# Attention stage: a group's choice of experts run one slot later, woven between the operations that add the next group's attention

## The chip, the core and the metric

The kernel runs on one core of a Trainium2 chip. Its metric is the device time of one execution in microseconds, as the median of several runs. The engines of the core have a queue each and work through it strictly in order: the matmul engine (PE in the profile), the Vector engine (DVE), the Scalar engine (ACT), GpSimd (POOL), and SP, which here only issues DMAs. Engines wait for each other, and an engine for its own earlier results, by semaphores.

## The reference

Four residual layers over 4096 tokens of width 128: linear attention, a mixture of 8 experts, a token mix with a decaying scan, and the same experts again. What the change touches is the attention and the choice of one expert for each token that follows it.

```python
def attn(x):                                 # x: 4 x 1024 x 128, normed
    q, k = elu(x @ W_q) + 1, elu(x @ W_k) + 1
    v = x @ W_v
    S, z = running sums over t of k_t v_t^T and of k_t
    return ((S_t q_t) / max(z_t . q_t, 1e-6)) @ W_o

def ffn(x):                                  # x normed
    logits = x @ router_W + router_b
    top1 = argmax(softmax(logits))           # one expert of 8
    gate = softmax(logits)[top1]
    return gate * (relu(x @ W1[top1] + b1[top1]) @ W2[top1] + b2[top1])

x = x + attn(layernorm(x))
x = x + ffn(layernorm(x))
x = x + mix(layernorm(x))
x = x + ffn(layernorm(x))
```

## The kernel before

The order on each engine is written out by hand. The 4096 tokens are 32 tiles of 128, and 4 tiles are a group (`GT = 4`, `NG = 8` groups). The attention stage is a software pipeline of slots k = 0 to 8: each engine has a function `attn_slot(k)` that does for several groups the steps whose turn it is.

In slot k PE does, in this order: `project_qk(k)` (L1271), `project_out(k-2)` (L1349, which gives the attention's output y of group k-2 with its denominator and its part of the logits), `score(k-1)` (L1286), `turn_kv(k-1)` (L1298, L1301), `transpose_x(k+1)` (L1246), the prefix counts `count` of group k-3 (L1256, L1260), `updates(k-1)` (L1310), `read_intra(k-1)` (L1321), `read_inter(k-1)` (L1332) and `project_v(k)` (L1276). Slot 8 has no `project_qk` and no `project_v`.

In slot k DVE does: the addition of the attention to the rows of group k-2, that is `dmax` (L891, which waits for y), `rden` (L894), `lnew` (L899) and four rows operations (L904); the moments of these rows (`stats` L802, L807); `mask_scores(k-1)` (`am`, L913); `add_state(k-1)` (L921 or L924); `placed(k-3)` (L867 to L878); `phi(k)` (L932); `scan_z(k)` (L939); and then `choose(k-2)`, which has eight small steps in a chain, each on the result of the one before it: `lsum` L836, `ls` L844, `lg` L847, `mx` L849, `ld` L852, `rv` L855, `top` L857, `oh` L858. In slot 8 the steps of the expert table (`slot_table`, first L1062) come right after `am`.

`read_intra(k-1)` needs `am(k-1)`, and `am(k-1)` stands on DVE's queue behind the addition and the moments of group k-2, hence behind y of group k-2.

POOL does in slot k: `z_dot_q(k-1)` (L484, reads two tiles of 64x512 in SBUF), `old_logits(k-2)` (L490), `row_scales(k-2)` (L476, waits for the moments through ACT's L619), and four indirect DMAs (L502), the second half of group k-4 and the first half of group k-3. In the kernel before, `z_dot_q(k-1)` also waits until `oh` of group k-3 is there (`after(pool, AS["oh"], k - 2)`). ACT copies and activates what PE made, and takes the exponential of `ld` (`lexp`, L612).

Of the kernel before, what the change touches and what calls it, by code (L numbers as in the profile page):

```python
# [5 lines left out]
ALU = mybir.AluOpType  # L6
# [6 lines left out]
P = 128  # L13
# [32 lines left out]
def after(eng, sem, n):  # L46

    if n > 0:
        eng.wait_ge(sem, n)
# [11 lines left out]
def hybrid_block(nc, x, w_q, w_k, w_v, w_o, time_decay, mix_v, mix_r, rw_v, rw_r, rw_o,  # L61
# [41 lines left out]
    with ExitStack() as ctx:  # L103
# [199 lines left out]
        def per_tile(a, n):  # L303
            return a.unsqueeze(2).to_broadcast([P, n, E])
# [111 lines left out]
        def _(pool):  # L416
# [123 lines left out]
            for k in range(NG + 1):  # L540
                if k == 2:
                    scales(AS, len(NORM_BATCHES) - 1)

                after(pool, AS["oh"], k - 2)
                if 0 <= k - 1 < NG:
                    z_dot_q(k - 1)
                if k == NG:
                    send(0, AS, k - 4, 1)
                if k - 2 >= 0:
                    old_logits(k - 2)  # L550
                    row_scales(AS, k - 2)
                if 4 <= k < NG:
                    send(0, AS, k - 4, 1)
                if k - 3 >= 0:
                    send(0, AS, k - 3, 0)
# [20 lines left out]
        def _(act):  # L576
# [44 lines left out]
            def phi_parts(g):  # L621
                act.wait_ge(AS["qkp"], g + 1)

                after(act, AS["phi"], g)
                nc.scalar.activation(ex[:], bank[1][:], ACT.Exp)
                nc.scalar.activation(rl[:], bank[1][:], ACT.Relu).then_inc(AS["rel"], 1)
# [38 lines left out]
            def attn_slot(k):  # L665
                if k < NG:
                    phi_parts(k)
                if k - 3 >= 0:
                    lexp(0, AS, k - 3)
                if 0 <= k - 1 < NG:  # L670
                    evac_kv(k - 1)
                if k == 0:

                    evac_xT(AS, 1, "vp")
                    turned_weights()
                    evac_v(0)
                    router_weights()
                    norm(AS, 2)
                    return
                if k == NG:  # L680
                    evac_o(k - 1)
                    row_veps(AS, k - 2)
                    copy_w1(0, 0)
                    return
                if k + 1 < NG:
                    evac_xT(AS, k + 1, "vp")
                if k - 2 >= 0:
                    row_veps(AS, k - 2)
                if k + 2 < NG:
                    norm(AS, k + 2)  # L690
                if 0 <= k - 1:
                    evac_o(k - 1)
                evac_v(k)
# [102 lines left out]
        def _(dve):  # L796
# [14 lines left out]
                dve.wait_ge(s_x_in[g], 16 * (l + 1))  # L811
                moments((AS, BS)[l], 1, g)

            def choose(l, S, b, half=None):

                t = span(ROUTE_BATCHES[b])
                n = GT * len(ROUTE_BATCHES[b])
                steps = 5 if l == 0 else 4
                done = [steps * b + (3 if l == 0 else 2) * (half == 1)]

                def step(ins):
                    done[0] += 1
                    ins.then_inc(s_route[l], 1)
                    dve.wait_ge(s_route[l], done[0])

                rev = rev8[:].unsqueeze(1).to_broadcast([P, n, E])
                if half != 1:
                    logits_of(l, S, b, t, n, step)
                if half != 0:
                    argmax_of(S, b, t, n, rev, step)  # L830

            def logits_of(l, S, b, t, n, step):
                dve.wait_ge(S["rs2"], b + 1)
                if l == 0:
                    dve.wait_ge(AS["lold"], ROUTE_BATCHES[b][-1] + 1)
                    step(nc.vector.tensor_tensor(lsum[:, t], lnew[:, t], lold[:, t], ALU.add))  # L836
                    sums = lsum[:, t]
                elif b == LASTB:
                    dve.wait_ge(S["lnew"], 1)
                    sums = lnew[:, t]  # L840
                else:
                    dve.wait_ge(S["logits"], ROUTE_BATCHES[b][-1] + 1)
                    sums = bank[6][:, 0:n * E].rearrange("p (j e) -> p j e", e=E)
                nc.vector.tensor_tensor(ls[:, t], sums, per_tile(column(RSTD, t), n), ALU.mult  # L844
                                        ).then_inc(S["lgs"], 1)
                dve.wait_ge(S["lgs"], b + 1)
                step(nc.vector.tensor_tensor(lg[:, t], ls[:, t], rtb[:].unsqueeze(1).to_broadcast([P, n, E]),  # L847
                                             ALU.add))
                step(nc.vector.tensor_reduce(mx[:, t], lg[:, t], AX_X, ALU.max))  # L849

            def argmax_of(S, b, t, n, rev, step):
                nc.vector.tensor_tensor(ld[:, t], lg[:, t], per_tile(mx[:, t], n), ALU.subtract  # L852
                                        ).then_inc(S["lead"], 1)
                dve.wait_ge(S["lead"], b + 1)
                step(nc.vector.scalar_tensor_tensor(out=rv[:, t], in0=ld[:, t], scalar=0.0, in1=rev,  # L855
                                                    op0=ALU.is_equal, op1=ALU.mult))
                step(nc.vector.tensor_reduce(top[:, t], rv[:, t], AX_X, ALU.max))  # L857
                nc.vector.tensor_tensor(oh[:, t], rev, per_tile(top[:, t], n), ALU.is_equal).then_inc(S["oh"], 1)  # L858

            def placed(l, S, b):  # L860

# [23 lines left out]
            def by_bank(a):  # L885
                return a.rearrange("p (b j) -> p b j", b=2)

            def denominators(g):
                t = tiles(g)
                dve.wait_ge(AS["y"], g + 1)  # L890
                nc.vector.tensor_scalar(by_bank(dmax[:, t]), outs[:, :, :, D], 1e-6, None, ALU.max  # L891
                                        ).then_inc(AS["dmax"], 1)
                dve.wait_ge(AS["dmax"], g + 1)
                nc.vector.reciprocal(rden[:, t], dmax[:, t]).then_inc(AS["rden"], 1)  # L894

            def add_attention(g):
                t = tiles(g)
                dve.wait_ge(AS["rden"], g + 1)
                nc.vector.tensor_tensor(lnew[:, t].rearrange("p (b j) e -> p b j e", b=2), outs[:, :, :, D + 1:YC],  # L899
                                        by_bank(rden[:, t]).unsqueeze(3).to_broadcast([P, 2, 2, E]), ALU.mult  # L900
                                        ).then_inc(AS["lnew"], 1)
                for j in range(GT):
                    v = val(g * GT + j)
                    last = nc.vector.scalar_tensor_tensor(out=v, in0=outs[:, j // 2, j % 2, 0:D],  # L904
                                                          scalar=rden[:, g * GT + j:g * GT + j + 1], in1=v,
                                                          op0=ALU.mult, op1=ALU.add)
                last.then_inc(AS["xnew"], 1)

            def mask_scores(g):
                dve.wait_ge(AS["scores"], g + 1)  # L910
# [31 lines left out]

            def attn_slot(k):

                if 0 <= k - 2:
                    denominators(k - 2)
                    add_attention(k - 2)
                if k == NG:

                    mask_scores(k - 1)  # L950
                    slot_table(0, 0, (0, 1))
                    add_state(k - 1)
                    slot_table(0, 0, (2,))
                if 0 <= k - 2:
                    dve.wait_ge(AS["xnew"], k - 1)
                    moments(AS, 2, k - 2)
                if 0 <= k - 1 < LASTG:
                    mask_scores(k - 1)
                    if k == 1:
                        mix_weights(1)  # L960
                    add_state(k - 1)
                if k - 3 >= 0:
                    placed(0, AS, k - 3)
                if k == NG:
                    return
                phi(k)
                scan_z(k)
                if k - 2 >= 0:
                    choose(0, AS, k - 2)
                if k < 2:  # L970
                    first_moments(0, k + 6)
                if k == 0:
                    mix_weights(0)
# [140 lines left out]
            def experts(l):  # L1114
# [39 lines left out]
                final = len(STAGES) - 1  # L1154
                dve.wait_ge(s_w2, 16 * (1 + E))
                if l == 0:
                    denominators(LASTG)
                    add_attention(LASTG)
                    norm_rows(0)
                else:  # L1160
                    norm_rows(0)
                    add_mix(LASTG)
# [428 lines left out]
```

## Time and profile before

| | us |
|---|---|
| median of 3 runs | 324.19 |
| lowest and highest run | 323.43, 325.46 |
| span of the profiled execution, first to last instruction | 351.4 |
| attention slots 2 to 8 in it, from the first to the last `dmax` | 23.30 to 74.69 |
| granted clock of the matmul engine in 26.8 to 77.0 | 1.00 |

The profiled execution gives no other time of its own than its span, which is 27.2 us longer than the median. The profile names a line as L904, an engine's idle time stands in brackets behind the instruction that ended it, and a count as x4 says that four instructions were merged into one row. The stage of interest is the attention, from about 5 to 83 us.

### The profile page before, as it was taken

The page shows a single profiled execution, that of the slowest core. Times are in us where ns is not written, and L with a number is a line of the kernel's source. Part 1 is how long each engine was busy: PE and PEld are TensorE (multiplying, and loading weights), DVE is VectorE, ACT ScalarE, POOL GpSimd, SP SyncE. Part 2 cuts the span into 40 slices and gives each one's busy share as a digit, 9 for nine tenths or more (in the row PEclk, how much of TensorE's full clock was granted, in tenths as well). Part 3 has the DMA queues.
Part 4 walks back from the last instruction along what each step waited for, and adds up shares of the span by engine and source line. Part 5 has one row for each costly group of instructions (what it writes and reads, how often), then busy time and mean ns, then how long its engine had stood idle before and what let it go on. Part 6 is the DMA issues. An engine that isn't in the chain of part 4 may idle for free.

```text
span 351.4 us, 9045 instructions
## 1 busy us (share of the span) xinstructions
PE 298.9 (85%) x2177; PEld 259.3 (74%) x2177; DVE 243.1 (69%) x1012; ACT 188.3 (54%) x545; POOL 205.9 (59%) x244
## 2 busy tenths in 40 slices
PE   7899998898948799999998978797976599989970
PEld 7566666655838799999945857686866499989960
DVE  4888989897563476877617999689453367777740
ACT  3865654323753576777604834423654377677730
POOL 4853688887565345545427867888483544544550
PEclk9999999999996899999999999968996899999995
DMA  7999010012223333310026000112212343321100
GB/s 194 272 322 142 20 34 31 31 33 79 64 62 94 76 79 82 90 52 32 23 67 172 2 16 15 48 39 79 67 59 78 79 87 83 89 57 40 33 7 0
DMA packets 32530, 25.72 MB, mean 73 GB/s; under 512 B 6000, under 2 KB 28785, under 8 KB 32480
## 3 DMA queue, kind: packets, MB, share of 16 engines
q1 hardware_dynamic: 27328, 16.51, 20.0%
q0 software_dynamic: 4576, 8.54, 7.4%
q8 instruction: 20, 0.33, 0.4%
q14 instruction: 30, 0.25, 0.2%
q10 hardware_dynamic: 576, 0.10, 0.2%
HBM read 14.57 MB, written 11.53 MB: 74 GB/s over the span
## 4 chain that ended last, share of the span: by engine, by line
PE 54%; DVE 15%; issue 9%; POOL 6%; another core or an unknown queue 5%; ACT 4%; DMA 2%; DVEq 1%; POOLq 0%; ACTq 0%; SPq 0%
PE pair L1496 19%; PE pair L1486 12%; PE bank L1486 6%; DVE stats L802 3%; PE bank L1474 2%; PE pair L1408 2%; POOL rstd L464 2%; PE pair L1349 1%; PE pair L1310 1%; PE pair L1321 1%; DVE rows L904 1%; DVE ys L1149 1%; PE pair L1276 1%; PE pair L1415 1%
## 5 line engine op out<-in xcount | busy, mean ns | idle before, releaser
L1496 PE MATMUL pair<-w2s,hT 128*128 x624 | 88.5, 287 | 3.5 <-issue 2.4
L1496 PEld LDWEIGHTS pair<-w2s,hT 128*128 128x128 f32 x624 | 80.1, 201 | 6.2 <-issue 5.8
L502 POOL DMA_INDIRECT sorted<-rows,place x64 | 68.5, 1071 | 26.8 <-issue 16.9
L1486 PE MATMUL pair<-xsT,w1s 128*128 128x128 f32 x432 | 62.2, 283 | 2.7 <-ACT xsT L740 2.1
L515 POOL DMA_INDIRECT out<-ys,xs x39 | 38.2, 981 | 40.3 <-DVE ys L1149 21.8
L515 POOL DMA_INDIRECT x_mid<-ys,xs x39 | 38.3, 983 | 39.2 <-DVE ys L1149 22.1
L1486 PEld LDWEIGHTS pair<-xsT,w1s 128*128 128x128 f32 x432 | 56.0, 198 | 3.7 <-issue 3.4
L1149 DVE SCALAR_TENSOR_TENSOR ys<-pair,xs 128x128 f32<-128x128 f32 x78 | 27.2, 349 | 43.3 <-PE pair L1496 24.9
L663 ACT COPY w1s<-w1all 128x516 f32 x78 | 49.0, 628 | 6.8 <-issue 3.4
L740 ACT COPY xsT<-bank 128x128 f32<-128x128 f32 x78 | 20.9, 268 | 58.7 <-PE bank L1474 31.9
L1128 DVE SCALAR_TENSOR_TENSOR xs<-b2b,xs 128x128 f32<-128x128 f32 x78 | 27.5, 352 | 21.4 <-DVE xsn L1120 15.0
L1486 PE MATMUL bank<-xsT,w1s 128*128 128x128 f32 x192 | 30.7, 295 | 11.9 <-issue 6.6
L1486 PEld LDWEIGHTS bank<-xsT,w1s 128*128 128x128 f32 x192 | 26.9, 209 | 13.1 <-issue 7.4
L1138 DVE TENSOR_SCALAR hT<-pair,w1s 128x128 f32<-128x128 f32 x112 | 34.1, 343 | 0.9 <-PE pair L1486 0.8
L802 DVE BATCH_NORM_STATS2 stats<-rows 128x6 f32<-128x128 f32 x128 | 27.5, 277 | 10.0 <-DMA rows<-x_mid 6.1
L746 ACT ACTIVATE hT<-pair,w1s 128x128 f32<-128x128 f32 x104 | 31.5, 375 | 1.1 <-issue 0.5
L746 ACT ACTIVATE hT<-bank,w1s 128x128 f32<-128x128 f32 x96 | 29.3, 379 | 0.0
L1120 DVE TENSOR_SCALAR xsn<-xs 128x128 f32<-128x128 f32 x78 | 27.0, 348 | 0.3
L476 POOL TENSOR_TENSOR rows<-veps,neg_half 128x4 f32<-128x4 f32 x16 | 18.5, 1159 | 9.6 <-ACT veps L619 9.4
L1474 PE MATMUL bank<-ident,xsn 128*128 128x128 f32 x78 | 22.0, 282 | 0.6 <-issue 0.4
L599 ACT ACTIVATE xn<-rows,nmr,rstd 128x128 f32<-128x128 f32 x30 | 12.4, 490 | 15.3 <-POOL nmr L469 15.3
L1408 PE MATMUL pair<-wx,xnT 128*128 128x256 f32 x64 | 17.5, 421 | 0.7 <-ACT xnT L607 0.7
(164 smaller groups left out, 493.0 us busy)
## 6 DMA issues: line engine op xcount, KB each, us to landing
xs<-sorted SPq DMA_DIRECT2D x78, 66.0 KB
w1all<-in_L_ffn_W_b SPq DMA_DIRECT2D x8, 258.0 KB
rows<-in_L_attn_a_x SPq DMA_DIRECT2D x8, 256.0 KB, 4.1
w2s<-in_L_ffn_W SPq DMA_DIRECT2D x8, 256.0 KB, 5.8
rows<-x_mid SPq DMA_DIRECT2D x8, 256.0 KB, 4.5
sorted<-pad SPq DMA_DIRECT2D x30, 66.0 KB, 3.4
sorted<-rows,place POOLq DMA_INDIRECT x64
x_mid<-ys,xs POOLq DMA_INDIRECT x39
```

The costliest lines, as they stand in the source:

```text
L502: pool.indirect_dma_start(sorted_rows[l], bass.IndirectOffsetOnAxis(ap=place[:, t:t + 1], axis=0), rows[:, t, :], None).then_inc(s_sent[l] ...
L515: pool.indirect_dma_start(x_new[l], bass.IndirectOffsetOnAxis(ap=xs[b][:, IDC:IDC + 1].bitcast(I32), axis=0), ys[b][:], None, bounds_check ...
L663: nc.scalar.copy(w1s[i % NW][:], w1all[:, bass.ds(e, 1), :].rearrange("p o f -> p (o f)")).then_inc(s_w1, 1)
L746: last = nc.scalar.activation(hT[i % NB][:, c], bank[2 + i % 2][:, c * P:(c + 1) * P], ACT.Relu, bias=w1s[i % NW][:, DF + c:DF + c + 1])
L802: last = nc.vector.bn_stats(stats[:, t], val(t))
L1120: nc.vector.tensor_scalar(xsn[i % NB][:], xs[b][:, 0:D], xs[b][:, MEAN:MEAN + 1], xs[b][:, RSTD:RSTD + 1], ALU.subtract, ALU.mult).then_in ...
L1128: nc.vector.scalar_tensor_tensor(out=xs[b][:, 0:D], in0=b2b[:, bass.ds(e, 1), :].rearrange("p o d -> p (o d)"), scalar=xs[b][:, GATE:GATE ...
L1138: last = nc.vector.tensor_scalar(hT[i % NB][:, c], bank[4 + i % 2][:, f:f + P], w1s[i % NW][:, DF + c:DF + c + 1], 0.0, ALU.add, ALU.max)
L1149: nc.vector.scalar_tensor_tensor(out=ys[b][:], in0=bank[6 + i % 2][:, 0:P], scalar=xs[b][:, GATE:GATE + 1], in1=xs[b][:, 0:D], op0=ALU.mul ...
L1474: nc.tensor.transpose(bank[0][:, 0:P], xsn[i % NB][:], ident[:]).then_inc(s_xsT, 1)
L1486: mm = nc.tensor.matmul(bank[2 + 2 * half + i % 2][:, c * P:(c + 1) * P], w1s[i % NW][:, f:f + P], xsT[i % NB][:], start=True, stop=True)
L1496: mm = nc.tensor.matmul(bank[6 + i % 2][:, 0:P], hT[i % NB][:, c], w2s[:, bass.ds(e, 1), c, :].rearrange("p o d -> p (o d)"), start=(c == ...
```

## The change

`choose` is cut into eight functions, one for each step, and in the attention stage `choose(k-2)`, which stood at the end of slot k, is gone. `choose_and_add(k-3, k-2)` stands at the start of slot k from k = 3: a step of the choice of group k-3 and an operation of the addition of group k-2 in turn. Each step's wait on the step before it now stands in front of that step (before, it stood right behind the step before it). On ACT `lexp(k-3)` is issued behind `evac_kv(k-1)`. On POOL the wait of `z_dot_q` for `oh` is removed. The choices of groups 6 and 7, which are made in the expert stage, and those of the second layer keep their order.

```diff
@@ POOL
             for k in range(NG + 1):
                 if k == 2:
                     scales(AS, len(NORM_BATCHES) - 1)
-
-                after(pool, AS["oh"], k - 2)
                 if 0 <= k - 1 < NG:
                     z_dot_q(k - 1)
@@ ACT attn_slot
                 if k < NG:
                     phi_parts(k)
+                if 0 <= k - 1 < NG:
+                    evac_kv(k - 1)
                 if k - 3 >= 0:
                     lexp(0, AS, k - 3)
-                if 0 <= k - 1 < NG:
-                    evac_kv(k - 1)
@@ DVE
+            def sum_logits(b):
+                t = span(ROUTE_BATCHES[b])
+                dve.wait_ge(AS["lold"], ROUTE_BATCHES[b][-1] + 1)
+                nc.vector.tensor_tensor(lsum[:, t], lnew[:, t], lold[:, t], ALU.add).then_inc(s_route[0], 1)
...
+            def lead_logits(l, S, b):
+                t = span(ROUTE_BATCHES[b])
+                dve.wait_ge(s_route[l], routed(l, b, (3, 2)[l]))
+                nc.vector.tensor_tensor(ld[:, t], lg[:, t], per_tile(mx[:, t], GT * len(ROUTE_BATCHES[b])), ALU.subtract
                                         ).then_inc(S["lead"], 1)
...
+            def choose_and_add(b, g):
+
+                sum_logits(b)
+                bounded_sums(g)
+                scale_logits(0, AS, b)
+                reciprocals(g)
+                bias_logits(0, AS, b)
+                new_logits(g)
+                max_logit(0, b)
+                new_rows(g, 0)
+                lead_logits(0, AS, b)
+                new_rows(g, 1)
+                rank_leaders(0, AS, b)
+                new_rows(g, 2)
+                top_rank(0, b)
+                new_rows(g, 3)
+                one_hot(0, AS, b)
@@ DVE attn_slot
-                if 0 <= k - 2:
-                    denominators(k - 2)
-                    add_attention(k - 2)
+                if k == 2:
+                    add_attention(0)
+                if k >= 3:
+                    choose_and_add(k - 3, k - 2)
...
                 phi(k)
                 scan_z(k)
-                if k - 2 >= 0:
-                    choose(0, AS, k - 2)
```

DVE at the border of two slots, before: the last five steps of a choice, then the addition of the next group and its moments.

```order
L849 TENSOR_REDUCE mx<-lg 128x4 [waits s_route0]
L852 TENSOR_TENSOR ld<-lg,mx 128x32 [waits s_route0]
L855 SCALAR_TENSOR_TENSOR rv<-ld,rev 128x32 [waits a_lead]
L857 TENSOR_REDUCE top<-rv 128x4 [waits s_route0]
L858 TENSOR_TENSOR oh<-rev,top 128x32 [waits s_route0]
L891 TENSOR_SCALAR dmax<-pair 128x4 [waits a_y]
L894 RECIPROCAL rden<-dmax 128x4 [waits a_dmax]
L899 TENSOR_TENSOR lnew<-pair,rden 128x32 [waits a_rden]
L904 SCALAR_TENSOR_TENSOR rows<-pair,rden,rows 128x128 x4
L802 BN_STATS stats<-rows 128x6 [waits a_xnew]
```

DVE at the same place in the changed kernel, from the fifth instruction of `choose_and_add` on; ahead of it stand `lsum`, `dmax` (which waits for y), `ls` and `rden`.

```order
L844 TENSOR_TENSOR lg<-ls,rtb 128x32 [waits a_lgs]
L931 TENSOR_TENSOR lnew<-pair,rden 128x32 [waits a_rden]
L850 TENSOR_REDUCE mx<-lg 128x4 [waits s_route0]
L937 SCALAR_TENSOR_TENSOR rows<-pair,rden,rows 128x128
L855 TENSOR_TENSOR ld<-lg,mx 128x32 [waits s_route0]
L937 SCALAR_TENSOR_TENSOR rows<-pair,rden,rows 128x128
L861 SCALAR_TENSOR_TENSOR rv<-ld,rev 128x32 [waits a_lead]
L937 SCALAR_TENSOR_TENSOR rows<-pair,rden,rows 128x128
L867 TENSOR_REDUCE top<-rv 128x4 [waits s_route0]
L937 SCALAR_TENSOR_TENSOR rows<-pair,rden,rows 128x128
L872 TENSOR_TENSOR oh<-rev,top 128x32 [waits s_route0]
L800 BN_STATS stats<-rows 128x6 [waits a_xnew]
```

Seven of the eight steps have moved from the near side of `dmax`, and of its wait for y, to the far side, between that wait and the moments.

POOL around one `z_dot_q` (L484) of the attention stage, as the difference of the two kernels.

```order
 L490 TENSOR_TENSOR lold<-kv,std 128x32 [waits a_rs1,a_kv]
 L476 TENSOR_TENSOR rows<-veps,neg_half 128x4 [waits a_ve2]
-L484 TENSOR_TENSOR op<-zT,qk 64x512 [waits a_phi,a_y,a_z,a_oh]
+L484 TENSOR_TENSOR op<-zT,qk 64x512 [waits a_y,a_phi,a_z]
 L490 TENSOR_TENSOR lold<-kv,std 128x32 [waits a_rs1,a_kv]
```

Nothing on POOL changes its place; `z_dot_q` no longer waits for the one-hot choice.

## Rows read from the trace of the kernel before

**Rows 1.** The page, its head.

```profile
span 351.4 us, 9045 instructions
```

**Rows 2.** Timeline of DVE in slots 4 and 5: start us, us, engine, line, operation, tiles.

```profile
44.28 0.19 DVE L876 TENSOR_REDUCE place<-pick 128x4 int32<-128x32 f32 x1
44.39 0.17 DVE L878 RECIPROCAL rows<-sm 128x4 f32<-128x4 f32 x1
...
47.60 0.19 DVE L855 SCALAR_TENSOR_TENSOR rv<-ld,rev 128x32 f32<-128x32 f32 x1
47.82 0.19 DVE L857 TENSOR_REDUCE top<-rv 128x4 f32<-128x32 f32 x1
...
48.66 0.16 DVE L891 TENSOR_SCALAR dmax<-pair 128x4 f32<-128x4 f32 x1 [0.42 <-issue]
...
49.17 1.12 DVE L904 SCALAR_TENSOR_TENSOR rows<-pair,rden,rows 128x128 f32<-128x128 f32 x4
50.32 0.87 DVE L802 BATCH_NORM_STATS2 stats<-rows 128x6 f32<-128x128 f32 x4
...
51.52 0.66 DVE L913 TENSOR_TENSOR am<-pair,causal 128x512 f32<-128x512 f32 x1
```

**Rows 3.** Timeline of PE: `project_out` of slot 6, `read_intra` of slot 6, `project_out` of slots 7 and 8.

```profile
55.82 1.10 PE L1349 MATMUL pair<-wox,op 128*128 128x137 f32 x8
...
60.98 1.09 PE L1321 MATMUL pair<-am,kv 128*64 128x128 f32 x8 [0.59 <-DVE am L913]
...
64.79 1.10 PE L1349 MATMUL pair<-wox,op 128*128 128x137 f32 x8
...
72.24 1.10 PE L1349 MATMUL pair<-wox,op 128*128 128x137 f32 x8
```

**Rows 4.** Timeline of DVE at the starts of slots 4, 6, 7 and 8.

```profile
40.13 0.16 DVE L891 TENSOR_SCALAR dmax<-pair 128x4 f32<-128x4 f32 x1
...
57.41 0.15 DVE L891 TENSOR_SCALAR dmax<-pair 128x4 f32<-128x4 f32 x1
...
60.27 0.66 DVE L913 TENSOR_TENSOR am<-pair,causal 128x512 f32<-128x512 f32 x1
...
65.92 0.16 DVE L891 TENSOR_SCALAR dmax<-pair 128x4 f32<-128x4 f32 x1 [0.42 <-issue]
...
68.79 0.66 DVE L913 TENSOR_TENSOR am<-pair,causal 128x512 f32<-128x512 f32 x1
...
74.69 0.15 DVE L891 TENSOR_SCALAR dmax<-pair 128x4 f32<-128x4 f32 x1
...
76.24 0.68 DVE L913 TENSOR_TENSOR am<-pair,causal 128x512 f32<-128x512 f32 x1
76.83 0.79 DVE L1062 SCALAR_TENSOR_TENSOR ntile<-posb,whole 1x8 f32<-1x8 f32 x1
```

**Rows 5.** Timeline of POOL: `z_dot_q` (L484) of slots 3, 4, 5, 6 and 8.

```profile
30.81 1.27 POOL L484 TENSOR_TENSOR op<-zT,qk 64x512 f32<-64x512 f32 x1 [3.22 <-DVE oh L858]
...
40.59 1.29 POOL L484 TENSOR_TENSOR op<-zT,qk 64x512 f32<-64x512 f32 x1
...
49.95 1.27 POOL L484 TENSOR_TENSOR op<-zT,qk 64x512 f32<-64x512 f32 x1
...
59.03 1.27 POOL L484 TENSOR_TENSOR op<-zT,qk 64x512 f32<-64x512 f32 x1
...
76.31 1.29 POOL L484 TENSOR_TENSOR op<-zT,qk 64x512 f32<-64x512 f32 x1
```

**Rows 6.** The tile `ntile`: line, count, duration in ns as min/median/max.

```profile
L1062 DVE SCALAR_TENSOR_TENSOR ntile<-posb,whole x6: 122/148/787, 76.8 to 279.1; 1x8 f32<-1x8 f32 x6
```

**Rows 7.** Timeline of POOL in the mix stage.

```profile
189.94 1.07 POOL L462 TENSOR_SCALAR veps<-mv 128x4 f32<-128x4 f32 x1
```

**Rows 8.** Timeline of DVE in the mix stage.

```profile
189.76 1.23 DVE L992 TENSOR_TENSOR_SCAN sc<-decay,xnT 128x512 f32<-128x512 f32 x1 [0.52 <-ACT xnT L607]
```

**Rows 9.** Timeline of ACT in slot 5.

```profile
50.62 0.37 ACT L639 COPY kv<-pair 128x256 f32<-128x256 f32 x1 [1.70 <-PE bank L1301]
```

More of the change, by code:

```diff
@@ L812, in first_moments, with routed, rev_of, scale_logits @@
                 moments((AS, BS)[l], 1, g)
-            def choose(l, S, b, half=None):
+            def routed(l, b, n):
+                return (5, 4)[l] * b + n
+            def rev_of(b):
+                return rev8[:].unsqueeze(1).to_broadcast([P, GT * len(ROUTE_BATCHES[b]), E])
+            def sum_logits(b):
+                t = span(ROUTE_BATCHES[b])
+                dve.wait_ge(AS["lold"], ROUTE_BATCHES[b][-1] + 1)
+                nc.vector.tensor_tensor(lsum[:, t], lnew[:, t], lold[:, t], ALU.add).then_inc(s_route[0], 1)
+            def scale_logits(l, S, b):
                 t = span(ROUTE_BATCHES[b])
                 n = GT * len(ROUTE_BATCHES[b])
[L818 to L832, printed above, removed]
                 dve.wait_ge(S["rs2"], b + 1)
                 if l == 0:
-                    dve.wait_ge(AS["lold"], ROUTE_BATCHES[b][-1] + 1)
-                    step(nc.vector.tensor_tensor(lsum[:, t], lnew[:, t], lold[:, t], ALU.add))
+                    dve.wait_ge(s_route[0], routed(0, b, 1))
                     sums = lsum[:, t]
@@ L845, in logits_of, with bias_logits @@
                                         ).then_inc(S["lgs"], 1)
+            def bias_logits(l, S, b):
+                t = span(ROUTE_BATCHES[b])
+                n = GT * len(ROUTE_BATCHES[b])
                 dve.wait_ge(S["lgs"], b + 1)
[L847 to L852, printed above, removed]
+                nc.vector.tensor_tensor(lg[:, t], ls[:, t], rtb[:].unsqueeze(1).to_broadcast([P, n, E]), ALU.add
+                                        ).then_inc(s_route[l], 1)
@@ new lines, in max_logit @@
+            def max_logit(l, b):
+                t = span(ROUTE_BATCHES[b])
+                dve.wait_ge(s_route[l], routed(l, b, (2, 1)[l]))
+                nc.vector.tensor_reduce(mx[:, t], lg[:, t], AX_X, ALU.max).then_inc(s_route[l], 1)
+            def lead_logits(l, S, b):
+                t = span(ROUTE_BATCHES[b])
+                dve.wait_ge(s_route[l], routed(l, b, (3, 2)[l]))
+                nc.vector.tensor_tensor(ld[:, t], lg[:, t], per_tile(mx[:, t], GT * len(ROUTE_BATCHES[b])), ALU.subtract
@@ L853, in argmax_of, with rank_leaders @@
                                         ).then_inc(S["lead"], 1)
+            def rank_leaders(l, S, b):
+                t = span(ROUTE_BATCHES[b])
                 dve.wait_ge(S["lead"], b + 1)
[L855 to L858, printed above, removed]
+                nc.vector.scalar_tensor_tensor(out=rv[:, t], in0=ld[:, t], scalar=0.0, in1=rev_of(b),
+                                               op0=ALU.is_equal, op1=ALU.mult).then_inc(s_route[l], 1)
@@ new lines, in top_rank, with one_hot @@
+            def top_rank(l, b):
+                t = span(ROUTE_BATCHES[b])
+                dve.wait_ge(s_route[l], routed(l, b, (4, 3)[l]))
+                nc.vector.tensor_reduce(top[:, t], rv[:, t], AX_X, ALU.max).then_inc(s_route[l], 1)
+            def one_hot(l, S, b):
+                t = span(ROUTE_BATCHES[b])
+                dve.wait_ge(s_route[l], routed(l, b, (5, 4)[l]))
+                nc.vector.tensor_tensor(oh[:, t], rev_of(b), per_tile(top[:, t], GT * len(ROUTE_BATCHES[b])),
+                                        ALU.is_equal).then_inc(S["oh"], 1)
@@ L860, in placed, with choose @@
+            def choose(l, S, b, half=None):
+                if half != 1:
+                    if l == 0:
+                        sum_logits(b)
+                    scale_logits(l, S, b)
+                    bias_logits(l, S, b)
+                    max_logit(l, b)
+                if half != 0:
+                    lead_logits(l, S, b)
+                    rank_leaders(l, S, b)
+                    top_rank(l, b)
+                    one_hot(l, S, b)
             def placed(l, S, b):
@@ L886, in by_bank, with bounded_sums @@
                 return a.rearrange("p (b j) -> p b j", b=2)
-            def denominators(g):
+            def bounded_sums(g):
                 t = tiles(g)
@@ L892, in denominators, with reciprocals, new_logits @@
                                         ).then_inc(AS["dmax"], 1)
+            def reciprocals(g):
+                t = tiles(g)
                 dve.wait_ge(AS["dmax"], g + 1)
                 nc.vector.reciprocal(rden[:, t], dmax[:, t]).then_inc(AS["rden"], 1)
-            def add_attention(g):
+            def new_logits(g):
                 t = tiles(g)
@@ L901, in add_attention, with new_rows @@
                                         ).then_inc(AS["lnew"], 1)
-                for j in range(GT):
[L903 to L907, printed above, removed]
+            def new_rows(g, j):
+                v = val(g * GT + j)
+                row = nc.vector.scalar_tensor_tensor(out=v, in0=outs[:, j // 2, j % 2, 0:D],
+                                                     scalar=rden[:, g * GT + j:g * GT + j + 1], in1=v,
+                                                     op0=ALU.mult, op1=ALU.add)
+                if j == GT - 1:
+                    row.then_inc(AS["xnew"], 1)
+            def add_attention(g):
+                bounded_sums(g)
+                reciprocals(g)
+                new_logits(g)
+                for j in range(GT):
+                    new_rows(g, j)
+            def choose_and_add(b, g):
+                sum_logits(b)
+                bounded_sums(g)
+                scale_logits(0, AS, b)
+                reciprocals(g)
+                bias_logits(0, AS, b)
+                new_logits(g)
+                max_logit(0, b)
[7 more added lines that the diff above has]
+                one_hot(0, AS, b)
             def mask_scores(g):
@@ L1156, in experts @@
                 if l == 0:
-                    denominators(LASTG)
                     add_attention(LASTG)
```

## The prediction

> **What bounds the kernel now.** I read the page first for the span [rows 1], then the timelines of DVE and PE side by side through the attention slots, then POOL's. The times between 23 and 83 us matter; the expert and mix stages keep their instructions. Each slot of the attention is named here by the `dmax` that opens it on DVE.
>
> The reader should look for a loop that runs through both engines. In slot 6 `am` ends at 60.27 + 0.66 = 60.93 [rows 4]; PE, which had been idle for 0.59 us for it, starts `read_intra` at 60.98 and goes without a gap through `read_inter`, `project_v`, `project_qk` and `project_out`, which ends at 64.79 + 1.10 = 65.89 [rows 3]. DVE, idle for 0.42 us, takes y at 65.92, adds the attention, takes the moments, masks the scores and ends the next `am` at 68.79 + 0.66 = 69.45 [rows 4]. So the loop is 4.99 us from `am` to y on PE and 3.53 us from y to `am` on DVE, 8.52 in all. Whatever DVE does between `am` and the next y is free as long as it fits into the 4.99; whatever stands between y and `am` is paid for in full.
>
> Before, the eight steps of a choice stand in the free part. Do they fit? In slots 5 and 7, and in slot 3 likewise, they do: `dmax` waits for y (the 0.42 in [rows 2, 4]). In slot 6 y was ready at 55.82 + 1.10 + 0.03 (the pace of slot 7) = 56.95 [rows 3] and `dmax` started at 57.41 without idle time [rows 4], so DVE's own queue held it by 0.46. In slot 8 y was ready at 72.24 + 1.10 + 0.03 = 73.37 [rows 3] against 74.69 [rows 4]: held by 1.32, since this slot has no `project_qk`. In slot 4 `dmax` starts without idle time too [rows 4]; I take nothing as masked there, and were it like slot 6 the sum below would be 0.46 less. What taking the steps out of the free part can give is therefore 0.46 + 1.32 = 1.78 us.
>
> **The change, part by part.** *Steps into the other part.* Two prices for a small DVE step are in the trace. `top` waits for `rv` and starts 0.22 after it; L878, whose input is older, starts 0.11 after L876 [rows 2]. So weaving does hide a step's latency: a small step on its own row of results costs 0.22, between others 0.11. Rows operations are 0.26 apart: four last 1.12, the last one's own length is 0.34, and (1.12 - 0.34) / 3 = 0.26. Before, from `dmax` to the first rows operation it is 49.17 - 48.66 = 0.51, and to `stats` 50.32 - 48.66 = 1.66 [rows 2]. After: `lsum` runs before y. From `dmax` on stand three pairs of small steps (`dmax`, `ls`; `rden`, `lg`; `lnew`, `mx`), each pair 0.22 since both chains have latency 0.22, so the first rows operation is at 0.66; then four pairs of a rows operation and a small step at 0.26 + 0.11 = 0.37, which gives 0.66 + 1.48 = 2.14 for `stats`. `ld` is then at 0.92, `rv` at 1.29, `oh` at 2.03. The paid part grows by 2.14 - 1.66 = 0.48 us in each of slots 3 to 8; before y, 1.8 us of work go, where only 0.46 and 1.32 of two slots were late.
>
> *The sum of that.* At y of slot 8: 5 slots (3 to 7) x 0.48 = 2.40, less 1.78, is +0.62. In slot 8 no moments stand between, `am` starts 76.24 - 74.69 = 1.55 after `dmax` [rows 4] and will start 2.14 after it: +0.59. Together +1.21 us when the table of the first expert stage begins.
>
> *POOL's `z_dot_q` (L484).* It reads 2 x 64x512 from SBUF in 1.27 to 1.29 us. It starts 0.46, 1.29, 1.62 and 1.62 after `dmax` in slots 4, 5, 6 and 8 (40.59 - 40.13; 49.95 - 48.66; 59.03 - 57.41; 76.31 - 74.69) [rows 2, 4, 5]; slot 7 is like slot 5. In that stretch DVE now has rows operations and moments, which go on as usual. But L1062, a step with two inputs in SBUF with a median of 0.148, took 0.787 once [rows 6]: it started at 76.83 and ended at 77.62, and L484 ended at 76.31 + 1.29 = 77.60 [rows 4, 5]. The other way round, POOL's L462 ended at 191.01 when DVE's scan with two SBUF inputs ended at 190.99, having taken 1.07 [rows 7, 8]. I read this as one port that the two engines hold in turn for a whole instruction. `ls`, `lg`, `ld`, `rv` and `oh` have two SBUF inputs each, and the change puts them exactly into that stretch.
>
> Where L484 will fall: it comes after POOL's four DMAs, which come after L476, which waits for the moments; `am` waits for them as well. So both move together, and L484's distance to y stays, except where y used to be masked: slot 6 becomes 1.62 + 0.46 = 2.08, slot 8 1.62 + 1.32 = 2.94. Slot 4: L484 covers 0.46 to 1.75, `ld` at 0.92 waits 0.83. Slots 5 and 7: L484 from 1.29 to 2.56, at the very moment of `rv`; if `rv` slips in first, `oh` waits 2.56 - 2.03 = 0.53, if not, `rv` waits 1.27; I take 0.90, the middle. Slot 6: 2.08 is just behind `oh` at 2.03; 0 or up to 1.27, and I take 0.4, nearer to the miss. Slot 8: L484 misses the choice and meets the table's steps, one of which waited 0.65 before; at 2.94 it can cost a whole 1.27, or as little as before plus 0; I take +0.35. Sum: 0.83 + 2 x 0.90 + 0.4 + 0.35 = 3.4; ends 0.83 + 2 x 0.53 = 1.9 and 0.83 + 3 x 1.27 + 0.6 = 5.2. DVE works in order, so `stats`, `am` and PE behind them are as late.
>
> *The rest at nothing.* The wait of `z_dot_q` for `oh` held POOL once, 3.22 us in slot 3 [rows 5]; L484 then starts at about 29, right behind its scan, before y of slot 3, and nobody waits for its result for another slot. From slot 4 on the DMAs ahead of it had set its time. Without that wait nothing keeps it off the choice; kept, it would have had to start behind `oh`. `lexp` on ACT: `ld` is now there only 0.9 to 1.8 us after y, and ACT idles 1.70 before `evac_kv` [rows 9]; behind that copy it delays nothing. `count` on PE now waits for `oh` at 2.03 to 3.3 after y, but the `am` behind it comes at 4.0 at the earliest, and its count and the updates fit between. `placed` finds `le` and the counts ready. SP's queue is the same.
>
> *A rule against the change.* The trace has 0.11 us between independent steps and 0.22 between dependent ones [rows 2]. The Trainium skill, VectorE: DVE Perf Modes, section "The DRAIN you can't avoid", says that the pipeline is flushed after every operation, so that semaphores between chained ones cost nothing extra. By that rule weaving would hide nothing; this trace disagrees.
>
> **The sum.** 1.2 + 3.4 = +4.6 us, made against the profiled execution: 351.4 [rows 1] becomes 356.0. That execution is 27.2 longer than the median of 324.19, and no row says where; I take the same 4.6 for the runs: 328.8, or +1.4%. Behind the attention PE's `project_out` of group 7 and the first loads hang on this end, so I count the delay as passed on.
>
> **The rivals.** *No contention for these steps:* only one DVE instruction in the trace was held, on one partition; if short 128x32 steps get through between POOL's reads, the rest stays: +1.2, 325.4. For it speaks that POOL may give up the port between pieces; against it the end of L1062 within 0.02 of L484's. *Faster, DVE is the limit:* if in the runs outside the profiler y comes earlier than DVE can take it in every slot, the choice leaves the limiting queue. A slot's choice and addition go from 8 x 0.22 + 1.66 = 3.42 to 0.11 + 2.14 = 2.25: 1.17 less, in six slots 7.0. It begins to win when y comes 0.5 us sooner in most slots; PE's share of the loop then soon binds again, so I take about half, -4, 320.2. Against it speak the idle 0.42 before `dmax`, and the granted clock of 1.00; for it the 27.2 us that I can't place. *No overlap of steps:* seven steps at 0.22 = 1.54 on the paid side in place of 0.48, six times: 1.2 + 6.4 = +7.6, 331.8. *It doesn't reach the end:* the first expert loads set the time anyway, 324.2.
>
> **How the numbers follow.** Contention 0.60 (own range 327.3 to 330.6, from +3.1 to +6.4), no contention 0.20, faster 0.12, no overlap 0.04, absorbed 0.04. One per cent, 3.2 us, is about what a measurement of this kernel can tell from no change. Faster by more: 0.10 of the 0.12. Slower by more: 0.54 of the 0.60 and the 0.04, 0.58. Within: 0.32. The range leaves out the faster case and the two small ones: 325.0 to 330.6.
>
> **What would show it.** In the profile after: `dmax` idle for y by 1 to 2 us in every slot from 3 on; `dmax` to `stats` at 2.1 where L484 is absent (slot 3) and 2.6 to 3.4 in slots 4, 5 and 7, with one of `ld`, `rv`, `oh` lasting up to 1.4 us and ending with L484; `am` to y unchanged at 4.99 in slot 7 and 56.95 - 52.18 = 4.77 in slot 6 (`am` of slot 5 ends at 51.52 + 0.66 [rows 2]); `dmax` of slot 8 near 78.3 where it was at 74.69. It would be wrong if `dmax` still starts without waiting, if all small steps last 0.19, or if the attention ends later and the expert stage starts at the old time.

## The result and the profile after

The changed kernel takes 338.4 us against 323.81, a ratio of 1.0435 (95% interval 1.0396 to 1.0474): 4% slower. The prediction was 328.8 with a range up to 330.6. The side was right, the size was not: 14.6 us where 4.6 were worked out. All ratios here compare fast executions alone (a few executions were over 1.5% slower than the fastest of their kernel), so they can differ a little from the ratio of the medians beside them.

Its profiled execution has a span of 336.6 us. That of before [rows 1] had 351.4, which is no measure of the change, because chips differ in the expert stages. On the chip of experiment 1 and of the first runs of experiments 2 to 4 the kernel before takes 354.19, on the others 323.8 to 325.5. The second profile of before, on the slow chip, has a span of 352.2 with the attention slots at the first profile's times (`dmax` of slot 8 at 74.89 against 74.69). Where one kernel was profiled on both kinds of chip, the attention agrees too: `dmax` of slot 8 at 75.15 and 75.00 in the two runs of experiment 2, at 81.06 and 81.14 in those of experiment 3. So the attention slots are compared across profiles, and whole times only on one chip.

DVE in slot 4, from the timeline of the profile after (start us, us, engine, line, operation, tiles; in brackets the idle time before). These lines answer to [rows 2, 4]:

```profile
40.55 0.16 DVE L920 TENSOR_SCALAR dmax<-pair 128x4 f32<-128x4 f32 x1 [1.65 <-PE pair L1406]
40.63 1.60 DVE L837 TENSOR_TENSOR ls<-lsum,rows 128x32 f32<-128x32 f32 x1
42.15 0.17 DVE L926 RECIPROCAL rden<-dmax 128x4 f32<-128x4 f32 x1
...
44.04 0.87 DVE L800 BATCH_NORM_STATS2 stats<-rows 128x6 f32<-128x128 f32 x4
...
45.24 0.66 DVE L972 TENSOR_TENSOR am<-pair,causal 128x512 f32<-128x512 f32 x1
...
54.69 0.16 DVE L920 TENSOR_SCALAR dmax<-pair 128x4 f32<-128x4 f32 x1 [5.61 <-PE pair L1406]
```

`ls`, which takes 0.19 in slot 3, lasts 1.60 and ends at 42.23. POOL's `z_dot_q` ends at 42.17, as its timeline shows (this answers to [rows 5]):

```profile
29.03 1.27 POOL L484 TENSOR_TENSOR op<-zT,qk 64x512 f32<-64x512 f32 x1 [1.43 <-DVE zT L998]
...
40.89 1.28 POOL L484 TENSOR_TENSOR op<-zT,qk 64x512 f32<-64x512 f32 x1
...
52.17 1.28 POOL L484 TENSOR_TENSOR op<-zT,qk 64x512 f32<-64x512 f32 x1
...
65.01 1.28 POOL L484 TENSOR_TENSOR op<-zT,qk 64x512 f32<-64x512 f32 x1
```

Two more steps are held in the same way, `rv` in slot 6 (ends at 66.35; `z_dot_q` at 66.29) and `ls` in slot 7:

```profile
63.46 0.16 DVE L920 TENSOR_SCALAR dmax<-pair 128x4 f32<-128x4 f32 x1 [1.65 <-PE pair L1406]
...
64.71 1.64 DVE L861 SCALAR_TENSOR_TENSOR rv<-ld,rev 128x32 f32<-128x32 f32 x1
...
68.20 0.66 DVE L972 TENSOR_TENSOR am<-pair,causal 128x512 f32<-128x512 f32 x1
...
74.78 0.16 DVE L920 TENSOR_SCALAR dmax<-pair 128x4 f32<-128x4 f32 x1 [2.89 <-PE pair L1406]
74.86 1.64 DVE L837 TENSOR_TENSOR ls<-lsum,rows 128x32 f32<-128x32 f32 x1
...
79.52 0.66 DVE L972 TENSOR_TENSOR am<-pair,causal 128x512 f32<-128x512 f32 x1
...
87.45 0.16 DVE L920 TENSOR_SCALAR dmax<-pair 128x4 f32<-128x4 f32 x1 [3.11 <-PE pair L1406]
```

The larger part is on PE. Its timeline from `am` of slot 4 to y of slot 5 answers to [rows 3]:

```profile
44.20 0.18 PE L1313 MATMUL pair<-oh,before 128*128 128x32 bf16 x1 [1.77 <-DVE rows L937]
...
45.95 1.97 PE L1378 MATMUL pair<-am,kv 128*64 128x128 f32 x8
47.85 1.97 PE L1389 MATMUL pair<-qk,state 64*64 64x128 f32 x8
49.75 1.98 PE L1333 MATMUL pair<-xnT,wc 128*72 128x512 f32 x2
51.52 1.91 PE L1328 MATMUL pair<-xnT,wc 128*128 128x512 f32 x2
53.23 1.43 PE L1406 MATMUL pair<-wox,op 128*128 128x137 f32 x8
```

PE is idle for 1.77 us, and then `read_intra` takes 1.97 us where it takes 1.09 in [rows 3]. The view by stages shows why (busy us and instructions of PE, PE's weight loads, DVE, ACT and POOL; then the granted clock, DMA share, GB/s). Two stretches of the profile after:

```profile
44.00:54.00 10.00, 9.79 (x35) 6.63 (x36) 4.86 (x20) 3.07 (x9) 6.88 (x7) 0.51 0.08 27
...
75.00:90.00 15.00, 12.75 (x72) 9.29 (x71) 10.81 (x46) 3.03 (x9) 10.05 (x12) 0.66 0.08 28
```

The first of them in the profile of before:

```profile
44.00:54.00 10.00, 9.30 (x75) 7.06 (x73) 8.56 (x38) 5.29 (x15) 8.12 (x9) 1.00 0.09 30
```

The granted clock is 0.51, that is the lower of its two levels (1.2 GHz), almost throughout 44 to 54; the kernel before holds 1.00 there. Cut into single microseconds, the same view has 0.50 in each from 44 to 53 and in each from 78 to 88, and a shorter stretch of it from 68 to 71. PE looks fully busy, 9.79 of 10.00 us, because its instructions take up to nearly twice as long (1.97 for 1.09), and it gets 35 of them done where before did 75. A busy share without the clock beside it would hide the loss.

### The profile page after: what moved, and what is told of

Same layout as the page of the kernel before. It is cut to its first block, busy times and chain, and to the rows that moved or that the text cites. A ratio compares the mean times of both kernels' runs of the same rounds, so it can differ in the third digit from the quotient of the medians.

```text
span 336.6 us, 9039 instructions
## 1 busy us (share of the span) xinstructions
PE 300.6 (89%) x2177; PEld 258.3 (77%) x2177; DVE 241.9 (72%) x1012; ACT 188.1 (56%) x545; POOL 204.5 (61%) x244
## 4 chain that ended last, share of the span: by engine, by line
PE 57%; DVE 21%; POOL 8%; issue 6%; DMA 3%; ACT 2%; DVEq 1%; POOLq 0%; SPq 0%
PE pair L1553 18%; PE pair L1543 13%; PE bank L1543 6%; DVE stats L800 4%; PE pair L1378 3%; PE pair L1406 3%; PE pair L1333 3%; POOL sorted L502 3%; PE pair L1389 2%; PE bank L1531 2%; POOL rstd L464 2%; DVE rows L937 2%; PE pair L1328 2%; PE pair L1367 2%; DVE ls L837 1%
## 5 line engine op out<-in xcount | busy, mean ns | idle before, releaser
L1553 PE MATMUL pair<-w2s,hT 128*128 x624 | 84.5, 279 | 3.3 <-issue 2.7
L502 POOL DMA_INDIRECT sorted<-rows,place x64 | 67.4, 1053 | 24.2 <-issue 16.8
L1553 PEld LDWEIGHTS pair<-w2s,hT 128*128 128x128 f32 x624 | 76.3, 193 | 6.5 <-issue 6.3
L1543 PE MATMUL pair<-xsT,w1s 128*128 128x128 f32 x432 | 60.0, 276 | 0.8 <-issue 0.4
L1543 PEld LDWEIGHTS pair<-xsT,w1s 128*128 128x128 f32 x432 | 53.8, 192 | 1.4 <-issue 0.9
L1543 PE MATMUL bank<-xsT,w1s 128*128 128x128 f32 x192 | 28.6, 282 | 0.4 <-ACT xsT L738 0.4
L1543 PEld LDWEIGHTS bank<-xsT,w1s 128*128 128x128 f32 x192 | 25.3, 198 | 0.6 <-ACT xsT L738 0.6
```

Of the source, the lines that this page charges most:

```text
L502: pool.indirect_dma_start(sorted_rows[l], bass.IndirectOffsetOnAxis(ap=place[:, t:t + 1], axis=0), rows[:, t, :], None).then_inc(s_sent[l] ...
L1543: mm = nc.tensor.matmul(bank[2 + 2 * half + i % 2][:, c * P:(c + 1) * P], w1s[i % NW][:, f:f + P], xsT[i % NB][:], start=True, stop=True)
L1553: mm = nc.tensor.matmul(bank[6 + i % 2][:, 0:P], hT[i % NB][:, c], w2s[:, bass.ds(e, 1), c, :].rearrange("p o d -> p (o d)"), start=(c == ...
```

## The experiments

**1. The kernel before, profiled again.** No edit. 

> The kernel before, unchanged, for a second profiled execution. The first has a span of 351.4 us against a median of 323.8, the changed kernel's has 336.6 against 338.4. If the first profile of before was disturbed outside the attention, this one has a span near 322, with the attention slots at the same times (dmax of slot 8 near 74.7) and the missing time in the expert stages. If the profiler always lengthens this kernel, it is near 351 again.

The span is 352.2, and the slots are where they were: `dmax` at 23.30, 31.82, 40.13, 48.65, 57.51, 66.03, 74.89. Neither of the two possibilities holds. The 13 executions of this kernel on this chip take 350.3 to 356.3 us, median 354.19, so it is the chip and not the profiler, and the attention isn't touched by it. That the first profile of before was taken on such a chip too is concluded from its equal span; it isn't on record. In 90 to 125 us, the first expert stage, PE did 179 instructions in the first run of experiment 2 and 288 in the second, the same kernel on two chips. What differs between the chips there wasn't looked into.

**2. The wait of `z_dot_q` kept.**

```diff
+                after(pool, AS["oh"], k - 2)
                 if 0 <= k - 1 < NG:
                     z_dot_q(k - 1)
```

> The changed kernel with one line put back: z_dot_q on GpSimd waits for the one-hot choice, as before. Theory 1 (DVE steps with two SBUF inputs are held by z_dot_q, PE idles longer for that, and its granted clock then falls): z_dot_q can't start before oh, no step lasts over 0.2 us, PE's idle time before count stays near 0.4, the clock stays at its upper level, dmax to stats is 2.1 in all slots: +1.2 us against before, 325. Theory 2 (the steps on the paid side lengthen PE's idle time enough by themselves to lower its clock): the clock falls all the same and the time stays above 332.

356.62 against 354.19, ratio 1.0078 (1.0035 to 1.0121). Again, on the chip where before takes 324.56:

> The changed kernel with z_dot_q's wait for oh put back, again. Theory 1: no hold in a choice, upper clock through slot 8: +1 to +3 us. A theory in which the clock falls by chance or because of the weaving itself: near the changed kernel.

326.52 against 324.56, ratio 1.0050 (1.0020 to 1.0080): +2 us of the changed kernel's +12.8. Both runs are far from what Theory 2 asked for. The timeline of DVE in this second run shows slot 4 without a hold:

```profile
40.47 0.16 DVE L921 TENSOR_SCALAR dmax<-pair 128x4 f32<-128x4 f32 x1 [1.65 <-PE pair L1407]
40.55 0.19 DVE L838 TENSOR_TENSOR ls<-lsum,rows 128x32 f32<-128x32 f32 x1
...
42.43 0.18 DVE L873 TENSOR_TENSOR oh<-rev,top 128x32 bf16<-128x32 f32 x1
42.55 0.87 DVE L801 BATCH_NORM_STATS2 stats<-rows 128x6 f32<-128x128 f32 x4
```

and POOL's, how the wait keeps `z_dot_q` behind the choice:

```profile
42.70 1.26 POOL L484 TENSOR_TENSOR op<-zT,qk 64x512 f32<-64x512 f32 x1 [1.92 <-DVE oh L873]
```

The clock in the same windows as above, from its view by stages:

```profile
44.00:54.00 10.00, 8.88 (x66) 6.70 (x67) 7.84 (x37) 5.92 (x18) 7.87 (x9) 1.00 0.09 30
75.00:90.00 15.00, 12.93 (x86) 8.90 (x87) 12.10 (x59) 5.36 (x17) 10.65 (x12) 1.00 0.26 70
```

So weaving alone neither holds a step of a choice nor lowers the clock up to `dmax` of slot 8, in either run. In ten us PE does 66 instructions where the changed kernel does 35. Behind the choices `z_dot_q` still meets the table's first step, as in the first profile of before, which is a part of the +2:

```profile
77.66 1.07 DVE L1121 SCALAR_TENSOR_TENSOR ntile<-posb,whole 1x8 f32<-1x8 f32 x1
```

In the first run this step lasts 1.16, and there the granted clock does fall afterwards, to 0.50 in 83 to 86 us; `dmax` of group 7 comes at 84.74 where the second run has it at 83.49.

**3. Filler matmuls ahead of `count`.** Their result isn't used; the rest is the changed kernel.

```diff
+                if 4 <= k < NG:
+                    for _ in range(6):
+                        nc.tensor.matmul(bank[2][:, 0:P], ident[:], ident[:], start=True, stop=True)
                 if 3 <= k < NG:
```

> The changed kernel with six more 128x128 matmuls on PE in each of slots 4 to 7, into a bank that is free then, behind the transposes, where PE would wait for count; their result is not used. Theory 1: the holds on DVE remain, about 1.5 us each in three to five slots, but PE is not idle in them and the clock stays: 1.2 + 3 to 6 us, so 328 to 331, 8 to 10 us faster than the changed kernel. If the lower clock is not due to PE's idle time, 338 as the changed kernel.

361.3 against 354.19, ratio 1.0215 (1.012 to 1.031). Again, beside the changed kernel:

> The changed kernel with six matmuls in each of slots 4 to 7 ahead of count, again. Theory 1: five holds of 1.45 us (PE on time brings z_dot_q to each choice), 7.3 us, and no lower clock in the slots: +7 to +9 us, so 5 to 7 us faster than the changed kernel beside it, although two more steps are held.

333.1 against 324.56, ratio 1.0248 (1.0210 to 1.0287), 4.2 us faster than the changed kernel (experiment 7) with 24 matmuls more; 5 to 7 were expected. From slot 4 on every slot's choice is now held once, as the timeline of DVE in the second run shows:

```profile
40.83 1.60 DVE L837 TENSOR_TENSOR ls<-lsum,rows 128x32 f32<-128x32 f32 x1
...
52.03 1.67 DVE L855 TENSOR_TENSOR ld<-lg,mx 128x32 f32<-128x32 f32 x1
...
62.60 1.65 DVE L861 SCALAR_TENSOR_TENSOR rv<-ld,rev 128x32 f32<-128x32 f32 x1
...
72.65 1.70 DVE L855 TENSOR_TENSOR ld<-lg,mx 128x32 f32<-128x32 f32 x1
...
83.11 1.78 DVE L872 TENSOR_TENSOR oh<-rev,top 128x32 bf16<-128x32 f32 x1
```

and the clock stays up, from the view by stages:

```profile
44.00:54.00 10.00, 8.92 (x70) 7.14 (x71) 7.88 (x31) 4.56 (x13) 6.86 (x7) 1.00 0.08 28
```

Microsecond by microsecond it is 1.00 up to 89 us. Five holds are 8.40 - 5 x 0.19 = 7.5 us. That separates the two losses: weaving and five holds without the lower clock cost 8.5 us in all, and PE kept busy in the wait keeps its clock.

**4. The kernel before with only the wait removed.**

```diff
-                after(pool, AS["oh"], k - 2)
                 if 0 <= k - 1 < NG:
                     z_dot_q(k - 1)
```

> The kernel before with only z_dot_q's wait for oh removed. Theory 1: z_dot_q moves in slot 3 alone, from 30.8 to about 29.0, where it meets lsum to oh of the first choice; one step there may be held for about 1.3 us, of which 1.09 are free before dmax: within 0.5 us of before. A rival, that this wait does more than it seems and its removal is the whole loss: near 338.

358.63 against 354.19, ratio 1.0118 (1.0031 to 1.0205). Theory 1, as I had put it, failed here; it says that nothing but slot 3 moves.

> The kernel before with only z_dot_q's wait for oh removed, again. In the first run one-hot steps at the end of a choice were held by 1.8 us in slots 4 and 8 and the clock fell once, dmax of slot 8 6.4 us later. If this comes with the removed wait, the time is 4 to 7 us above before here as well; if it was a chance of that execution, it is at before.

328.19 against 324.56, ratio 1.0112 (1.0074 to 1.0151), a loss of 3.6 us (2.4 to 4.9 by the interval), where 4 to 7 were expected. In the second run's timelines of DVE and of POOL:

```profile
29.49 1.14 DVE L843 TENSOR_TENSOR ls<-lsum,rows 128x32 f32<-128x32 f32 x1
...
40.27 1.96 DVE L857 TENSOR_TENSOR oh<-rev,top 128x32 bf16<-128x32 f32 x1
42.15 0.15 DVE L890 TENSOR_SCALAR dmax<-pair 128x4 f32<-128x4 f32 x1
```

```profile
39.88 0.99 POOL L502 DMA_INDIRECT sorted<-rows,place  x1 [0.30 <-issue]
40.89 1.28 POOL L484 TENSOR_TENSOR op<-zT,qk 64x512 f32<-64x512 f32 x1
```

`oh` is issued 0.62 us before the recorded start of `z_dot_q` and is held until 42.23 all the same. So the recorded start comes later than the moment from which `z_dot_q` shuts DVE out. In the kernel before the two stand in the same way, `oh` 0.61 us before the recorded start of 40.59 [rows 5], and `oh` is not held:

```profile
39.98 0.19 DVE L858 TENSOR_TENSOR oh<-rev,top 128x32 bf16<-128x32 f32 x1
```

```profile
39.58 0.99 POOL L502 DMA_INDIRECT sorted<-rows,place  x1 [0.30 <-issue]
```

With and without the wait, the recorded start lies 0.02 behind the end of the DMA ahead of it. The wait did not set that start; it kept `z_dot_q` from shutting DVE out before `oh` was done. Nor is it the DMA that holds DVE: before, `oh` runs at full speed inside it. The hold of `ls` at 29.49 is free, as it fits into the idle time before `dmax` of slot 3. Behind the one of `oh`, `dmax` of slot 5 comes at 53.76 where it came at 48.66, with the lower clock again:

```profile
44.00:54.00 10.00, 9.19 (x42) 6.30 (x39) 6.07 (x27) 3.71 (x10) 6.87 (x7) 0.66 0.08 28
```

**5. A stall on DVE without contention.** The kernel before, with 24 operations more whose results aren't used (`STALLS` is 8).

```diff
                     denominators(k - 2)
+                    if k in (4, 6, 7):
+                        for i in range(STALLS):
+                            nc.vector.bn_stats(idle6[:, STALLS * k + i], causal[:])
                     add_attention(k - 2)
```

> The kernel before with eight moment operations on a constant tile, results unused, behind dmax in slots 4, 6 and 7, about 1.65 us in each: DVE is late by a hold's length there, with no contention and no moved step. If a late DVE lets PE idle and so lowers its clock, the time is far above the stalls' sum: 3 x 1.65 - 0.46 = 4.5 us for these, and 3 to 9 us more for the clock: 331 to 337. If only the stalls count: 328.3.

332.52 against 325.46, ratio 1.0174 (1.0128 to 1.0221). That is 5.7 us (4.2 to 7.2), between the 4.5 expected for the stalls alone and the 7.5 or more with the clock: the time doesn't tell the two apart. The four executions differ, and the longer ones have the lower mean clock: 330.39, 331.51, 333.54 and 335.74 us at 0.968, 0.963, 0.954 and 0.947. The profile, of the execution with 333.54, does tell them apart. In the timelines of DVE and of POOL in slot 4:

```profile
40.28 0.16 DVE L893 TENSOR_SCALAR dmax<-pair 128x4 f32<-128x4 f32 x1
...
40.58 1.62 DVE L951 BATCH_NORM_STATS2 idle<-causal 128x6 f32<-128x128 f32 x8
...
44.55 0.66 DVE L915 TENSOR_TENSOR am<-pair,causal 128x512 f32<-128x512 f32 x1
```

```profile
40.76 1.28 POOL L486 TENSOR_TENSOR op<-zT,qk 64x512 f32<-64x512 f32 x1
```

Eight operations with one input each run right through `z_dot_q`, 0.2 us apart; none is held. And from `am`'s end at 45.21 to `dmax` of slot 5 at 53.39 it takes 8.18 us in place of 4.99. The view by stages:

```profile
44.00:54.00 10.00, 9.19 (x41) 6.38 (x41) 5.95 (x27) 3.74 (x10) 6.86 (x7) 0.66 0.08 28
```

A late DVE by itself is enough to lower PE's clock. Each stall makes `am` 1.40 later; the same stall in slot 6 did not lower it (4.99 from `am` to y), those in slots 4 and 7 did (8.18 in place of 4.99, and 6.79 in place of 3.92).

**6. Only the last choice woven.** The changed kernel with the wait kept, the choices of groups 0 to 4 at the ends of their slots again, and group 5's woven into slot 8.

```diff
+                after(pool, AS["oh"], k - 2)
                 if 0 <= k - 1 < NG:
                     z_dot_q(k - 1)
...
-                if k == 2:
-                    add_attention(0)
-                if k >= 3:
+                if 2 <= k < NG:
+                    add_attention(k - 2)
+                if k == NG:
                     choose_and_add(k - 3, k - 2)
...
+                if 2 <= k < NG - 1:
+                    choose(0, AS, k - 2)
```

> The changed kernel with the choices of groups 0 to 4 back at the end of their slots, GpSimd's wait for oh kept, and only the last one (group 5) woven into slot 8, where DVE's queue had held dmax by 1.32 us. Both theories: dmax of slot 8 starts 1.3 us earlier, the paid part grows by 0.6: -0.7 us, 323.1 against 323.8; z_dot_q behind oh then lies beside the table's steps and may hold one by up to 1.3, +0.6.

324.32 against 325.46, ratio 0.9986 (0.9960 to 1.0013): no difference that these runs can tell. `dmax` of slot 8 does start early, at 73.15, but `z_dot_q` holds the first step of the table, for longer than in the first profile of before (0.79); in the second it wasn't held (0.14). The timeline of DVE:

```profile
73.15 0.16 DVE L921 TENSOR_SCALAR dmax<-pair 128x4 f32<-128x4 f32 x1 [0.67 <-PE pair L1409]
...
75.81 1.06 DVE L1123 SCALAR_TENSOR_TENSOR ntile<-posb,whole 1x8 f32<-1x8 f32 x1
```

**7. The changed kernel on the chip of the repeated runs.** No edit. 

> The changed kernel itself, to stand beside the next three on one chip, since chips differ by up to 9% in the expert stages (before: 324 on one, 354 on another). Theory 1 (holds of about 1.45 us, and the clock that falls behind them): +4.4% where before takes 324 us, +4.0% where it takes 354; three holds and 8 us at the lower clock in the attention slots.

337.33 against 324.56, ratio 1.0408 (1.0358 to 1.0458): +12.8, as expected. On this one chip the parts can be put in a row: weaving with the wait kept +2.0; weaving, five holds, upper clock +8.5; the changed kernel, with three holds and the lower clock, +12.8; no weaving and no wait +3.6. In its profile the hold in slot 6 did not lower the clock, as its timeline of DVE shows:

```profile
67.37 0.66 DVE L972 TENSOR_TENSOR am<-pair,causal 128x512 f32<-128x512 f32 x1
...
73.03 0.16 DVE L920 TENSOR_SCALAR dmax<-pair 128x4 f32<-128x4 f32 x1 [1.99 <-PE pair L1406]
```

## Why the prediction was right in side and wrong in size

**The loop through both engines: right.** In every slot from 3 on `dmax` waits for y, 1.65 to 5.61 us; I had expected 1 to 2. From `dmax` to `stats` slot 3, which has no hold, takes 33.92 - 31.84 = 2.08; I had 2.14, since a small step behind a rows operation costs 0.10 and not 0.11. Weaving hides a step's latency, but on the side of y where time is paid for. The term of +1.2 us was measured, in experiment 2, as +2.0 (0.6 to 2.6 by the interval of the ratio) and on the other chip as +2.4 (1.2 to 4.3), which doesn't contradict it.

**The rule on chained operations.** Pairs of small steps are 0.22 apart in the woven part, as one chain's steps are before, and the paid part grew by 2.08 - 1.66 = 0.42 us. Had every step cost its full 0.22 there, it would have been 7 x 0.22 = 1.5. The Trainium skill, VectorE: DVE Perf Modes, section "The DRAIN you can't avoid", says that the next operation doesn't start until the pipeline is empty; for steps that don't depend on each other this trace disagrees. The same section adds that an operation that isn't held starts earlier, which the prediction left out and the trace bears out.

**The holds: right in kind, under-sized.** I had 0.83 + 0.90 + 0.4 + 0.90 in slots 4 to 7. In the profile after there are three, 1.41 + 1.45 + 1.45 = 4.3 us (1.60, 1.64, 1.64 less 0.19); slot 5 has none because PE's lower clock had delayed y past `z_dot_q`. With PE on time, experiment 3, every slot from 4 on has one of 1.4 to 1.6. The step that failed here is that I let a hold last from `z_dot_q`'s recorded start: steps issued 0.3 to 0.6 us ahead of that were held too, so even what looked like a near miss is a hit, and a hold is longer than the 1.27 that I took as its upper end. Still, the sum of the holds came out only 0.9 above my 3.4. The Trainium skill, SBUF — State Buffer, section "Who interferes with whom", says that a DVE instruction with two SBUF inputs contends with a GpSimd instruction that reads SBUF, that one with a single SBUF input doesn't, and that the shared pair of ports is an exclusive lock, by which the later of the two is fully blocked. Experiments 3, 4 and 5 agree: holds of up to 1.97 - 0.19 = 1.78 us for two inputs and none for one. Only the order can't be read from recorded starts: the steps held here are recorded as the earlier ones.

**"The rest at nothing": the wait for `oh`.** I wrote that from slot 4 on the DMAs ahead of `z_dot_q` had set its time. Its recorded start they did set, and it stayed 0.02 behind them when the wait went (experiment 4). But in slot 4 the wait had kept `z_dot_q` from shutting DVE out before `oh` was done: with the wait alone removed `oh` lasts 1.96, and the kernel loses 3.6 us, the lower clock behind that hold included. In [rows 5] `z_dot_q` starts at 40.59, 0.4 after `oh` ends, and I read that as a wait that costs and does nothing, since no idle time was shown.

**The missing term, the largest, and the step that put the forecast out of its range: PE's clock.** I noted the clock at 1.00, took `am` to y as unchanged (4.99 in slot 7) and so priced PE's longer idle time at nothing. From `am`'s end to the next `dmax` the loop was 4.99 on PE (3.92 into slot 8). In the profile after it is 54.69 - 45.90 = 8.79 in slot 5, 74.78 - 68.86 = 5.92 in slot 7 and 87.45 - 80.18 = 7.27 in slot 8: 3.80 + 0.93 + 3.35 = 8.1 us.

**The sum as it came out,** at `dmax` of slot 8: 5 x 0.42 - 1.78 = 0.3, holds 4.3, clock 8.1, together 12.7; measured 87.45 - 74.69 = 12.76. The second profile of the changed kernel (experiment 7) adds up too: its slots begin 0.2 late, holds 4.4, clock 2.79 + 0.01 + 3.36 = 6.2, with the 0.3 together 11.1; measured 85.78 - 74.69 = 11.1. In slot 8 `am` is another 0.5 later, and L1062 loses its old hold of 0.65 (0.14 after), where I had added 0.35; the second profile of before has no such hold either, so it had been a thing of one execution. `project_out` of group 7 starts at 94.22 in place of 81.12, 13.1 later, and the kernel takes 14.6 more; on the chip of experiment 7, 12.8. That a delay at the attention's end is passed on held within that; where the 1.5 us between these numbers lie isn't shown.

**The rivals.** No contention for these steps: false, three were held. DVE as the limit: false, since with all choices woven and none held (experiment 2) `dmax` waits for y in every slot and the kernel gains nothing. No overlap of steps: false, 0.42 where it asked for 1.54. It doesn't reach the end: false, +12.8 and +14.6.

**What stays open.** Which idle time lowers the clock. A stall of 1.40 us did in slots 4 and 7 of experiment 5 and did not in slot 6, though PE sat idle before `count` for the same 1.20 us in slots 4 and 6. The hold in slot 6 of the changed kernel, with 1.82 us of idle time before `count`, cost 0.93 us through the clock in one execution, and in the other PE took 73.03 - 68.03 = 5.00 there. So the length of that one gap doesn't decide it.

## What to carry to other kernels

Before a step is moved across a wait, find the loop that the wait belongs to: steps ahead of it may be free, and behind it even hidden latencies are paid for. A wait that seems to cost nothing can be what keeps two engines from holding each other up, so test its removal alone. And a late producer of PE is not priced by its lateness only: where PE has nothing else to do, look at the granted clock behind the gap.

## What was not expected of the hardware

- `z_dot_q`, a GpSimd operation with two SBUF inputs, shut DVE's steps with two SBUF inputs out from up to 0.63 us before its recorded start until 0.06 us behind its recorded end (experiment 4).
- One hold or stall of 1.4 to 1.8 us on DVE could cost 2.8 to 3.8 us more on PE, about twice itself, through a granted clock of 0.50 for the 7 to 10 us that followed; others, in slot 6, cost 0 to 0.9. Six 128x128 matmuls in each gap prevented it.
- Two chips differ by 9% on the same kernel (354.19 and 324.56), with the attention slots up to `dmax` of slot 8 within 0.2 us (experiments 2 and 3).
